# Local streams rebuilt in a four-stream transformer kernel: keys padded by ScalarE copies, rotary sines from PSUM, probabilities normalised by halves of the heads, and a new order of work

## The reference, cut to what matters

```python
def _layer(x, wqkv, qs, ksc, wo, lg, lb, w1, b1, w2, b2):
    h = shift_token(x)                       # second half of the features comes from the row before
    q, k, v = jnp.split(h @ wqkv, 3, axis=-1)        # 8 heads of 64
    q = l2norm(q) * qs
    k = l2norm(k) * ksc
    q, k = rotary_xpos(q, k)                 # q*cos*scale + rotate_half(q)*sin*scale; k with 1/scale
    o = local_attention(q, k, v)             # each row sees at most 64 rows back
    x = x + o @ wo
    h = shift_token(x)
    h = layernorm(h) * lg + lb
    a, g = jnp.split(h @ w1 + b1, 2, axis=-1)
    return x + (a * gelu(g)) @ w2 + b2
```

## Time and profile before

| what | value |
|---|---|
| time, median of 3 runs | 3358.2 us (3350.9 to 3362.22) |
| the profiled execution's own time | 3367.69 us |
| its span, first to last instruction | 3366.0 us |
| TensorE clock granted, mean of the span | 0.970 |
| busy share of the span: PE, DVE, ACT, POOL | 91%, 73%, 65%, 49% |
| DMA, mean | 26 GB/s |

### The profile page before, as it was taken

The page is one execution under the profiler, slowest core; times in us unless marked ns, Lnnn a source line. Parts: engine busy times, 40 slices in busy tenths (PEclk is TensorE's granted clock), DMA queues, the critical chain, the costliest instruction groups (busy, mean ns, idle before and its releaser), DMA issues.

```text
span 3366.0 us, 61815 instructions
## 1 busy us (share of the span) xinstructions
PE 3047.4 (91%) x20480; PEld 2183.1 (65%) x20480; DVE 2441.8 (73%) x5890; ACT 2200.7 (65%) x6084; POOL 1661.0 (49%) x1741
## 2 busy tenths in 40 slices
PE   4678999999999999999999999999999999988764
PEld 2455776666777766667677766667676766665543
DVE  4355778778777777788777787787777877866543
ACT  2345777767676767676777777676777776765532
POOL 1033555555545455555555555555454555554522
PEclk9789999999999999999999999999999999999877
DMA  2000111111111101111111111111111111110000
GB/s 69 21 18 19 23 24 29 31 30 24 31 25 23 31 23 31 31 24 31 30 26 23 25 29 31 30 25 31 25 23 25 29 31 31 24 23 20 13 15 10
DMA packets 113643, 88.64 MB, mean 26 GB/s; under 512 B 27274, under 2 KB 112692, under 8 KB 113332
## 3 DMA queue, kind: packets, MB, share of 16 engines
q1 hardware_dynamic: 113332, 84.68, 11.1%
HBM read 9.17 MB, written 4.19 MB: 4 GB/s over the span
## 4 chain that ended last, share of the span: by engine, by line
PE 52%; DVE 24%; POOL 10%; issue 5%; ACT 5%; DMA 3%; SPq 1%; DVEq 0%; POOLq 0%; ACTq 0%
DVE negmax L860 10%; POOL rn L625 6%; PE bank L1196 5%; PE bank L1180 5%; PE bank L1069 5%; PE bank L1088 4%; PE bank L1124 4%; PE bank L1134 4%; PE bank L1204 3%; DVE rawA L941 3%; PE bank L1188 3%; PE bank L1016 3%; POOL rawQ L620 2%; PE bank L1158 2%; PE bank L1151 2%
## 5 line engine op out<-in xcount | busy, mean ns | idle before, releaser
L696 ACT ACTIVATE probs<-bank 128x512 f32<-128x512 f32 (+1 forms) x1024 | 478.1, 573 | 205.9 <-PE bank L1069 205.4
L860 DVE TENSOR_REDUCE negmax<-bank 128x2 f32<-128x512 f32 (+1 forms) x896 | 564.8, 682 | 45.3 <-PE bank L1048 27.0
L576 POOL TENSOR_TENSOR veps<-moments,eps_tile 128x2 f32<-128x2 f32 x192 | 37.6, 196 | 938.5 <-DVE moments L809 938.5
L620 POOL TENSOR_TENSOR rawQ<-rawQ,rawP 128x512 f32<-128x512 f32 x256 | 347.4, 1357 | 182.0 <-DVE rawP L927 153.3
L625 POOL TENSOR_TENSOR rn<-ss,minus_half 128x16 f32<-128x16 f32 x128 | 425.1, 3321 | 7.6 <-DVE ss L934 7.5
L1124 PE MATMUL bank<-wqkv_sb,hS 128*128 128x512 f32 x768 | 379.4, 612 | 4.7 <-ACT hS L657 1.7
L1069 PE MATMUL bank<-qT,kT 128*128 128x256 f32 x2048 | 341.6, 301 | 27.7 <-issue 14.0
L1069 PEld LDWEIGHTS bank<-qT,kT 128*128 128x128 f32 x2048 | 278.6, 193 | 98.1 <-ACT qT L679 42.2
L596 POOL TENSOR_SCALAR_AFFINE_SELECT probs<-probs 128x256 f32<-128x256 f32 x512 | 231.5, 480 | 220.4 <-ACT probs L696 217.4
L954 DVE TENSOR_REDUCE negmax<-bank 128x2 f32<-128x384 f32 (+1 forms) x384 | 221.2, 595 | 129.5 <-PE bank L1151 115.5
L1088 PE MATMUL bank<-probs,V 128*16 128x256 f32 (+1 forms) x4096 | 249.7, 358 | 30.1 <-ACT probs L696 27.5
(11 more groups left out here) (158 smaller groups left out, 7797.4 us busy)
## 6 DMA issues: line engine op xcount, KB each, us to landing
kT<-rawC SPq DMA_DIRECT2D x256, 128.0 KB, 2.6
kT<-rawP SPq DMA_DIRECT2D x128, 256.0 KB, 3.9
xin<-x SPq DMA_DIRECT2D x32, 128.0 KB, 2.2
out<-xout SPq DMA_DIRECT2D x32, 128.0 KB, 2.2
V<-Y SPq DMA_DIRECT2D x32, 63.5 KB
V<-XY SPq DMA_DIRECT2D x32, 63.5 KB
wqkv_sb<-wqkv SPq DMA_DIRECT2D x1, 1536.0 KB
w_sb<-w SPq DMA_DIRECT2D x1, 682.0 KB
```

The source lines that it names most:

```text
L620: nc.gpsimd.tensor_tensor(cosine2[:, l, n, :], cosine2[:, l, n, :], two_in_P0[:, l, n, :], ALU.add)\
L696: nc.scalar.activation(dst, src, ACT.Exp, scale=SCALE0 if k == ATTN0 else SCALE1)\
L860: nc.vector.reduce_max(negmax[:, k, t, h0:h0 + nh], tile(u)[:, :].rearrange("p (h k) -> p h k", h=nh), AX.X, negate=True).then_inc(has_emp ...
```

## The change

It does these things, in streams 2 and 3:

1. `turn_k2`: ScalarE copies each half of the partitions straight from the bank into its padded place in `kT2`. That is two copies of 64 partitions where one of 128 was, and the two DMAs are gone, with the semaphore `k_in` that TensorE waited for.
2. `qkv2`: VectorE makes the sines itself in this unit, reading the raw values from the bank, not from SBUF. It waits for ScalarE's raw copy first (`raw_ready`), and it is VectorE that now frees the bank. The squares lie in a free part of `P1`.
3. `rope2` becomes `cos2` and `add2`: the cosine product is made in place in `rawA` or `rawB`, and the sum too. Each of the four parts has its own place for the sines, so parts 2 and 3 no longer wait for `scale2`.
4. `norm2` works on heads 0 to 3 and then 4 to 7, each for both halves of the rows; `scores2` comes in the order 0, 2, 3, 1, 4, 5; the transposes of probabilities 0 to 3 wait for the first half alone.
5. The semaphore `resid` of streams 1 to 3 is gone: who waited for it waits for the bank instead, and VectorE no longer waits for its own instruction there. The two DMAs of `shift_rows` change places. GpSimd's small set-up memsets come last.
6. `TURNS`, `BEGINS` and `BANKS` are new (220 units instead of 212).

```diff
-BEGINS = (33, 39, 29, 16)
+BEGINS = (23, 34, 25, 9)
 TURNS = {
     "tensor": (
-        "22200200222222333333122111120100003333331102222000"
+        "33220022111223333300032222112222200222002201333333"
...
-    units += [rope(0), norms(0), rope(1), scale(0), rope(2), norms(1), scale(1), rope(3), scale(2), scale(3)]
+    units += [qkv(0), cosine(0), qkv(1), cosine(1), norms(0), qkv(3), add(0), scale(0), qkv(4), add(1), scale(1),
+              cosine(2), cosine(3), qkv(2), qkv(5), norms(1), add(2), scale(2), add(3), scale(3)]
     units += [Unit("turn_q2", u, bank=1) for u in range(2)]
-    units += [Unit("turn_k2", u, bank=1, k_in=2 * 16 * u) for u in range(2)]
-    units += [Unit("scores2", u, bank=1, max_done=1) for u in range(6)]
+    units += [Unit("turn_k2", u, bank=1) for u in range(2)]
+    units += [Unit("scores2", u, bank=1, max_done=1) for u in (0, 2, 3, 1, 4, 5)]
...
-        cosine2 = rawQ[:, :, :].rearrange("p l (u n) -> p l u n", u=2)
+        sines = [rawQ[:, :, :].rearrange("p l (u n) -> p l u n", u=2), two_in_P0]
+        squares = [P1[:, :, :, WINDOW * (m + 1):WINDOW * (m + 2)] for m in range(2)]
...
-                elif u.kind == "turn_k2" and u.part == 1:
...
-                    for e in range(2):
-                        half = slice(64 * e, 64 * e + 64)
-                        sp.dma_start(kT2[half, l, :, e, :], two_in_P0[half, l].rearrange("p u (g q) -> p (u g) q", g=2))\
-                            .then_inc(sig("k_in", u), 16)
...
+                elif u.kind == "cos2":
+                    pool.wait_ge(sig("raw_ready", src), so_far("raw_ready", k, src, pas, j) + 1)
+                    nc.gpsimd.tensor_tensor(raw, raw, tab, ALU.mult).then_inc(sig("cos_part", u), 1)
+                elif u.kind == "add2":
...
+                    nc.gpsimd.tensor_tensor((q2, k2)[m][:, l, t, :], (q2, k2)[m][:, l, t, :], sines[m][:, l, t, :], ALU.add)\
                         .then_inc(sig("rot_sum", u), 1)
...
+                elif u.kind == "turn_k2":
+                    act.wait_ge(has_filled(u), uses(u, pas, j))
+                    for e in range(2):
+                        half = slice(64 * e, 64 * e + 64)
+                        last = nc.scalar.activation(kT2[half, l, 2 * u.part:2 * u.part + 2, e, :],
+                                                    tile(u)[half].rearrange("p (a q) -> p a q", a=2), ACT.Copy)
+                    last.then_inc(has_emptied(u), 1)
...
+                    nc.vector.reduce_sum(ss[:, l, t, m, :], squares[m][:, l], AX.X).then_inc(sig("sums", u), 1)
+                    dve.wait_ge(sig("raw_ready", u), so_far("raw_ready", k, u, pas, j) + 1)
+                    raw = tile(u)[:].rearrange("p (h d) -> p h d", h=HEADS)
...
                     nc.vector.tensor_tensor(sn[:, :, 32:64], raw[:, :, 0:32],
                                             tab[:, 32:64].unsqueeze(1).broadcast_to([P, HEADS, 32]), ALU.mult)\
-                        .then_inc(sig("sin_part", u), 1)
+                        .then_inc(has_emptied(u), 1)
...
+                    nc.vector.reciprocal(recip[:, k, :, own], expsum[:, l, :, own]).then_inc(sig("rec_done", u), 1)
                     dve.wait_ge(sig("rec_done", u), so_far("rec_done", k, u, pas, j) + 1)
+                    for t, part, n in ((0, P0[:, l, own], P), (1, P1[:, l, own, WINDOW:SEQ], SEQ - WINDOW)):
+                        last = nc.vector.tensor_tensor(part, part, recip[:, k, t, own].unsqueeze(2).broadcast_to([P, 4, n]), ALU.mult)
+                    last.then_inc(sig("p_ready", u), 1)
...
-                        pe.wait_ge(sig("k_in", u), so_far("k_in", k, u, pas, j))
-                        needs += of("turn_q2", 0, 1)
+                        needs += of("turn_q2", 0, 1) + of("turn_k2", 0, 1)
...
-                    if u.part == 0:
-                        pe.wait_ge(sig("p_ready", u), so_far("p_ready", k, u, pas, j))
+                    if u.part % 4 == 0:
+                        made = earlier(pas, u, "norm2", u.part // 4)
+                        pe.wait_ge(sig("p_ready", made), so_far("p_ready", k, made, pas, j) + 1)
```

More of the change, by code:

```diff
@@ L150, in local_units, with qkv, cosine, add @@
     units = [Unit("shift", bank=1)]
-    units += [Unit("qkv2", n, bank=1, **(dict(sq_ready=1, sums=1) if n % 3 < 2 else {})) for n in range(6)]
-    def rope(u):
-        return Unit("rope2", u, cos_part=1, sin_part=1, rot_sum=1)
+    def qkv(n):
+        return Unit("qkv2", n, bank=1, **(dict(sq_ready=1, sums=1, raw_ready=1) if n % 3 < 2 else {}))
+    def cosine(u):
+        return Unit("cos2", u, cos_part=1)
+    def add(u):
+        return Unit("add2", u, rot_sum=1)
     def norms(t):
@@ L175, in local_units @@
               turn_p(6), turn_p(7), mix2(2), mix2(3)]
-    units += [Unit("project2", bank=1, resid=1)]
+    units += [Unit("project2", bank=1)]
     units += [Unit("shift_rows", rows_in=2 * 16, rows_left=1)]
@@ L180, in local_units @@
     units += [Unit("up2", c, bank=1, gelu_done=1) for c in range(len(HTILES))]
-    units += [Unit("down2", bank=1, plus_bias=1, resid=1)]
+    units += [Unit("down2", bank=1, plus_bias=1, **({} if last else {"handed": 1}))]
     units += [Unit("finish", out_ready=1) if last else Unit("carry", carried=1)]
@@ L599, in unit @@
                 elif u.kind in ("down0", "down2"):
[L601 to L602 removed]
+                    if k == ATTN0:
+                        pool.wait_ge(sig("resid", u), so_far("resid", k, u, pas, j))
+                        made = []
+                    else:
+                        made = [taken(earlier(pas, u, "project2"))]
+                    for sem, count in newest(pas, j, *made, taken(earlier(pas, u, "turn"), 0)):
                         pool.wait_ge(sem, count)
@@ L810, in unit @@
                 elif u.kind == "shift_rows":
-                    dve.wait_ge(sig("resid", u), so_far("resid", k, u, pas, j))
+                    for sem, count in newest(pas, j, taken(earlier(pas, u, "project2"))):
+                        dve.wait_ge(sem, count)
                     nc.vector.tensor_copy(h[k][:, :, 0:64], Y[l][:, :, 0:64])
```

169 lines of the change are left out of this document (78 added, 91 removed).

## The result

| | before | after |
|---|---|---|
| time, median (4 runs each, side by side) | 3356.4 us | 3204.6 us (3203.6 to 3205.7) |
| ratio to before, 95% interval | | 0.9545 (0.953 to 0.956) |
| span of the profiled execution | 3366.0 us | 3202.6 us |
| filling, to the fifth residual sum | 395.1 us | 372.9 us |
| the 27 passes behind it | 2578.5 us, 95.5 each | 2474.2 us, 91.6 each |

The forecast was 3305 us in a range of 3245 to 3362. Of the 163.4 us that the span lost, 22.2 lie in the filling, 104.3 in the full passes and 36.9 in the draining; all three come from the starts of one line that runs once a pass.

A forecast was written before the change was run, and what follows sets the result against it. The prediction took the full passes as bound by PE and the draining by latency; ends -31 and full passes -22 made -53, from 3358.2 to 3305 us, with a range of 3245 to 3362.

The forecast's parts named there:

- The bound of the full passes: Full passes, PE-bound: at most PE's idle time, 3.16 us a pass or -88 in 28; expected -0.8 a pass, -22.
- The order costed at nothing: New order of work in the full passes: could move the time in either direction, no row tells, so no term.
- the order closes PE's gaps: Rival for the full passes: the new order fills some 2.5 us of PE's idle time a pass; 3257 us, chance 0.13.
- The ends: Filling and draining together, from shorter local waits and the row DMAs: -31 us, bounds -15 to -45.
- The filling: Start of the pipeline, one local sequence alone on its way: one key and one probability gain, -5 us.
- Sines from the bank: VectorE's sines reading PSUM at 420 ns: 71 us off DVE in the span, 2.2 a pass, 0.35 of the pass.
- 38 us less gained: Sines from the bank under the skill's PSUM access cost: an estimated 33 us more busy time, 38 us less gained.
- PE's other work hides it in full passes: ScalarE's extra key copies, 2.4 us a pass: hidden in full passes, costing the whole 2.4 if uncovered.
- Bank time as nothing: Banks with raw q or k held until the sines are made, at least 0.84 us longer: nothing in the sum.
- The rival: Banks held too long: PE stops at units whose bank awaits DVE's sines, 2 us a pass; 3383 us, chance 0.14.
- The row DMAs: `shift_rows`, large DMA issued second: 0.4 us later on each of about three on the chain, +1 us.

The follow-up runs named there:

- e13: Kernel before, order kept, with VectorE's maxima over 64 columns of each head and its sums of squares over 16 of 64: 3323.0 us, ratio 0.988.
- e15: Kernel before with VectorE's lighter maxima and sums, and ScalarE's attention exponentials over 128 of 512 columns: 3303.9 us, ratio 0.983.
- e9: Order and banks of before with all edits except the sines from the bank (they read an SBUF constant, ScalarE frees the bank): 3329.3 us, ratio 0.990 to before.
- e14: Changed kernel, order kept, with the same lighter VectorE maxima and sums as e13: 3151.1 us, ratio 0.938 to before.
- e5: Changed kernel with the sines reading a constant in SBUF and ScalarE's copy freeing the bank: 3419.4 us, ratio 1.017 to before.
- e2: Changed kernel with only the sines' input put into SBUF (a constant), VectorE still freeing the bank: 3430.9 us, ratio 1.020 to before.
- e10: Kernel before, in its own order, with only the key edit (ScalarE copies the keys into place, no key DMAs): 3369.8 us, ratio 1.002.
- e11: e9 with the two key DMAs put back: 3331.3 us, ratio 0.991 to before.
- e7: All edits, including the sines from the bank, with the order and banks of before: 3701.8 us, ratio 1.102 to before.
- e12: Changed kernel with the two row-shift DMAs in their old sequence, the large one first: 3202.7 us.
- e1: Changed kernel, order kept, with the keys put back to one ScalarE copy per bank and two DMAs: 3693.2 us, ratio 1.100 to before.
- e6: New order and banks with four edits undone (key DMAs, sines from SBUF, normalisation by halves of rows, `scale2` wait): 4178.4 us, ratio 1.244 to before.

## Why the prediction was wrong where it counted

**The bound of the full passes failed, and it is the error that counts.** The prediction had the direction and most of the local waits, but this step was wrong. It reads "what is to be had there is at most its idle time, plus whatever short waits the modelled ends of matmuls conceal", and the sum then used the idle time alone: the bound was -88 us for its 28 passes, and the term -22. Measured are 28 x 3.87 = -108, and 3.2 of 3.87 us a pass came out of busy time. The light kernels show that busy time holds waits for the other engines (0.97 us a pass in e13, 1.5 in e15); where the whole 3.2 came from stays open, as said above. The Trainium skill (Perfetto Trace Analysis, Identifying the Most-Contended Engine) warns that matmul busy time is not a good measure of the distance to the limit, and names the weight-load share as one to use in its place. This case's traces agree that busy time misleads: PEld was 66.6 of 95.5 us a pass and is 66.0 of 91.6, so it moved by 0.6 while busy fell by 3.2. In the earlier trace rows that number stood beside the other, and I did not use it.

**The order costed at nothing failed with it.** "That the order is new could move this in either direction, and no row tells it" was true, but then the range should have been open to both. The rival "the order closes PE's gaps" (3257 us, 0.13) named the right part of the change but not what it did: it had 2.5 us of listed idle time filled in a pass, and 0.65 were. It was held by the same false bound. The edits without the order and without the sines from the bank give 34 us (e9), so the other 118 of the 152 hang on the order, on the sines from the bank and on what the order lets the edits do.

**The ends were too small by nearly half.** I had -27 for the draining, -5 for the filling and +1, so -31 and at most -45. Measured are -36.9 and -22.2, of which one pass (3.9) belongs to the prediction's 28: about -55, outside the bound. The mechanisms in the draining were right, and their sizes near. In the last sequence the rotary part ends 6.1 us earlier (from the first cosine to the query transposes, 24.1 to 18.0, where I had 7.5), and from there to the transposed probabilities it is 7.9 us less (21.4 to 13.5), where I had 3.6 + 1.6. The filling was mis-sized by 13 to 17 us, where I had counted one key and one probability. e13 and e14, with lighter maxima and sums, shorten it by 21 us from before and 11 from after, so VectorE's work lies bare in part of it; e9 shortens it by 5.8, as forecast, without the new order and the sines from the bank.

**Sines from the bank: the busy time was right, its worth was not.** The four groups went from 286.3 to 211 us, a gain of 75 where I had 71. At the medians the rows hold, too: 414 ns from the bank. (The prediction's "38 us less gained" is a slip: its own numbers, 71 and 33, give 33 less, and 38 left.) But I took the gain as 2.2 us of DVE a pass, and 0.35 us of the pass for it. Under the new order the same edit is worth 7 us of DVE a pass (e5) and 226 us of time (e2), because that order puts the sines where GpSimd is at work.

**"PE's other work hides it in full passes" failed for ScalarE's copies, in small.** They take 0.59 us each, as priced (0.61), 2.4 us a pass. e10 shows a pass 0.3 us longer with them and e9 against e11 0.5; over 26 passes that takes about all that the ends gain by the missing DMA. That the copies are the cause is argued, not shown.

**Bank time as nothing** was about right for the order that came with the change (11 us, e2 against e5; 2.1 us of listed waits in the full passes). In the old order it would have been wrong: the sines' hold is PE's longest listed wait in e7, 5.3 us a pass, in a kernel 372 us slower than e9. The rival was right in kind: it would have decided, had the order not been laid anew. **The row DMAs**, +1, lie under what can be measured (e12).

## What to carry to other kernels

Where an order is written out by hand for a structure, an edit and its order are one change: undoing one edit at a time then prices what the order leans on (29 to 489 us here), and only the same edit in the old order shows what it gives alone (nothing, for the keys). Do not bound a gain by the idle time of an engine whose ends are modelled; read a measure beside it that does not move with the waits, and leave the range open where an order is new. An edit that shifts work from a DMA to a busy engine can gain at the ends and lose in the middle, as here, so price both.

## What the runs showed that I had not expected

- Time recorded as busy on TensorE shrank by 118.5 us of 3047.4 with the same 20480 matmuls.
- The granted clock in the stretch from 700 to 2400 us was 0.94 with the bare key DMA (e1), where PE is busy 88% of it, and 0.91 with all four edits undone (e6, 80%), against 1.00 in the full passes of the kernel after (97%): these means are mixes of its two levels, 2.4 and 1.2 GHz, so part of the price of a wait there is the clock.
- A VectorE product of 128x256 with two inputs in SBUF took 926 ns at the median in the new order (e5, q) and 415 in the old one (e9), at the same shape, and every one over 600 ns, 213 in e5 and 75 in e9, ran beside a GpSimd instruction. The Trainium skill (SBUF — State Buffer, Who interferes with whom) gives the rule for it, named in the prediction, and both traces agree.
